# Third graph layer: 64-row halves of the array for a unit's sums and its image's sums, the 65th column apart

## What is computed

```python
log_ij = _logmap(x[:, None, :], x[None, :, :], c)
agg = jnp.einsum('ij,ijc->ic', adj / deg, log_ij)
transformed = agg @ weight + bias
return _expmap(jnp.zeros_like(transformed), transformed, c)
```

## Time and profile before

| what | value |
|---|---|
| three runs | 1090.72, 1091.84, 1092.6 us, median 1091.84 |
| profiled execution, its own time | 1090.43 us |
| its span, first to last instruction | 1088.7 us |
| PE busy | 1036.7 us (95%), 5430 passes |
| DVE busy | 862.8 us (79%) |
| ACT busy | 767.5 us (71%) |
| mean granted clock of PE | 0.987 |

### The profile page before, as it was taken

One profiled execution on the slowest core, in us unless ns is written; L12 is line 12 of the kernel. 1 busy time (PEld: TensorE's weight loads), 2 busy tenths in 40 slices (PEclk: granted clock), 3 DMA queues, 4 the chain that ended last, 5 costly groups with the idle time before them and its releaser, 6 DMA issues.

```text
span 1088.7 us, 14887 instructions
## 1 busy us (share of the span) xinstructions
PE 1036.7 (95%) x5430; PEld 448.2 (41%) x5430; DVE 862.8 (79%) x1013; ACT 767.5 (71%) x807; POOL 270.7 (25%) x140
## 2 busy tenths in 40 slices
PE   7999999999789999999979999999999998989998
PEld 2333333336633333334324443444554554436544
DVE  7999989996766666697669987887789887898781
ACT  5555455553556656676688899988888888997682
POOL 1089500000010000003015364434343433440010
PEclk9999999999989999999999999999999999999999
DMA  9989989980048888778754445555455545446451
GB/s 353 396 343 423 393 322 346 359 331 30 2 154 274 280 290 280 247 274 288 245 180 136 135 135 175 177 172 193 155 168 181 170 140 174 136 140 208 140 173 40
DMA packets 96341, 238.32 MB, mean 219 GB/s; under 512 B 16400, under 2 KB 45072, under 8 KB 79888
## 3 DMA queue, kind: packets, MB, share of 16 engines
q1 hardware_dynamic: 87056, 220.62, 58.3%
q10 hardware_dynamic: 9216, 16.78, 4.0%
HBM read 219.55 MB, written 17.83 MB: 218 GB/s over the span
## 4 chain that ended last, share of the span: by engine, by line
PE 74%; DVE 12%; ACT 9%; issue 4%; DMA 1%; SPq 0%; DVEq 0%; ACTq 0%
PE PS L563 51%; PE PS L737 5%; PE PS L738 5%; PE PS L870 4%; PE PS L839 4%; ACT work L1224 2%; ACT work L1232 2%; DVE work L1969 2%; DVE work L1957 1%; ACT work L1235 1%; DVE ring L1975 1%; DVE work L1963 1%; ACT work L1218 1%; PE PS L575 1%; ACT work L1155 1%
## 5 line engine op out<-in xcount | busy, mean ns | idle before, releaser
L1637 DVE TENSOR_TENSOR work<-work,ring 128x1024 f32<-128x1024 f32 x128 | 151.2, 1223 | 76.8 <-ACT work L1155 76.7
L1155 ACT ACTIVATE work<-PS,att_sc 128x1024 f32<-128x1024 f32 x128 | 147.7, 1202 | 85.7 <-PE PS L738 78.4
L1090 ACT ACTIVATE work<-PS 128x1024 uint8<-128x1024 f32 x128 | 124.0, 1020 | 107.6 <-PE PS L563 107.6
L563 PE MATMUL PS<-ring,work 128*65 128x256 f32 (+1 forms) x600 | 191.8, 467 | 4.1 <-DVE work L1996 4.0
L541 POOL TENSOR_TENSOR ring<-work,ring 128x1024 f32<-128x1024 f32 x57 | 135.9, 2384 | 236.6 <-DVE work L1969 236.5
L563 PE MATMUL PS<-work 128*64 128x512 f32 (+2 forms) x800 | 153.6, 526 | 1.1 <-ACT work L1218 1.0
L1963 DVE SCALAR_TENSOR_TENSOR work<-PS,work 128x1024 f32<-128x1024 f32 x72 | 88.0, 1223 | 53.8 <-PE PS L563 45.3
L563 PEld LDWEIGHTS PS<-ring,work 128*65 128x65 f32 x600 | 80.8, 139 | 91.5 <-issue 66.0
L737 PE MATMUL PS<-work 128*128 128x512 f16 x256 | 98.9, 386 | 2.0 <-DVE work L1444 1.3
L1224 ACT ACTIVATE work<-work 128x1024 f32<-128x1024 f32 x72 | 76.0, 1055 | 34.8 <-DVE work L1957 34.7
L738 PE MATMUL PS<-work 128*128 128x512 f16 x256 | 98.2, 384 | 0.0
(11 more groups left out here) (267 smaller groups left out, 1479.9 us busy)
## 6 DMA issues: line engine op xcount, KB each, us to landing
ring<-in_adj_t SPq DMA_DIRECT2D x96, 1024.0 KB, 5.3
ring<-in_adj_t SPq DMA_DIRECT2D x104, 512.0 KB, 3.8
work<-in_adj_t SPq DMA_DIRECT2D x32, 1024.0 KB, 8.3
codes<-work ACTq DMA_DIRECT2D x64, 256.0 KB, 7.4
ring<-codes SPq DMA_DIRECT2D x64, 256.0 KB, 3.7
H<-in_adj_t SPq DMA_DIRECT2D x24, 512.0 KB, 3.9
X<-in_x SPq DMA_DIRECT2D x2, 256.0 KB, 4.5
X<-in_x SPq DMA_DIRECT2D x1, 512.0 KB, 9.9
```

Source lines behind the costliest of these rows:

```text
L563: return mm(out_ap, lhsT, rhs, start=starts, stop=True, skip_group_check=True)
L1090: nc.scalar.activation(made[:, k, u * UNIT:(u + 1) * UNIT], PS[:, (4 + 2 * u) * BANK:(6 + 2 * u) * BANK], ACT.Relu).then_inc(sem("codes_ma ...
L1155: nc.scalar.activation(att[:, u, :], PS[:, (4 + 2 * u) * BANK:(6 + 2 * u) * BANK], ACT.Sigmoid, bias=att_sc[:, 2:3], scale=att_sc[:, 1:2]) ...
L1637: V.tensor_tensor(prob[:, m % 4, :], att[:, u, :], ring[:, s % RING, u * UNIT:(u + 1) * UNIT], ALU.mult)\
```

## The change

A unit's near sums go to PSUM rows 0 to 63 of bank 2, its image's sums to rows 64 to 127 of bank 3, each product with 64 stationary columns instead of 65, and the two kinds alternate in program order. The 65th column gets products of its own with one stationary column: for a unit four near ones of 256 moving columns (rows 0 and 32 of the upper half of bank 3), for an image eight of 128 columns (rows 64 and 96). GA then keeps near sums in rows 0 to 63 and far sums in rows 64 to 127, and DVE adds up the 65th column apart (33 rows). `nodes2` adds the two halves with a stacked identity (made once by POOL) and fetches the 65th column with products of one moving column, one for each tile below 4 and two for each other tile. `turn_left(1)` moves from bank 3 to bank 0.

```diff
+        stacked = sb("stacked", [P, D])
...
+        GU = (work[:, 11 * UNIT:12 * UNIT], TA[:, 2 * UNIT:3 * UNIT])
+        LAST = 3 * BANK + PAIR
+        def last_near(S):
+            return GU[S // (NS // 2)][0:33, S % (NS // 2) * PAIR:(S % (NS // 2) + 1) * PAIR]
+        def last_far(p):
+            return GU[p // NS][64:97, p % NS * P:(p % NS + 1) * P]
+        def last_rows(t):
+            S, p = t // ST, t // 2
+            r = 32 * (t % ST // 2)
+            rows = [(r, GU[S // (NS // 2)][:, S % (NS // 2) * PAIR + t % 2 * P:S % (NS // 2) * PAIR + (t % 2 + 1) * P])]
+            if t >= ST:
+                r = 64 + 32 * (t % 2)
+                rows.append((r, GU[p // NS][:, p % NS * P:(p % NS + 1) * P]))
+            return rows
...
+            nc.gpsimd.tensor_tensor(stacked[:, :], ident[:, 0:D], ident[:, D:P], ALU.add).then_inc(sem("consts_ready"), 1)
...
-            pe.wait_ge(sem("consts_ready"), 6)
+            pe.wait_ge(sem("consts_ready"), 7)
...
                 if n == AUX_L:
-                    pe.wait_ge(sem("far_out"), mirrors(n - 1))
-                    turn_left(1, 3)
+                    pe.wait_ge(sem("aux_r_out_a"), 2)
+                    turn_left(1, 0)
...
                 if n > AUX_R and mirrors(n) == mirrors(AUX_R) + 1:
-                    pe.wait_ge(sem("aux_r_out_a"), 2)
+                    pe.wait_ge(sem("aux_l_out"), 2)
                     pe.wait_ge(sem("aux_r_out_v"), 2)
...
-            def gather2_near(n):
+            def gather2(n):
...
+                if mirrored(n):
+                    pe.wait_ge(sem("far_ready"), mirrors(n))
+                if mirrors(n) - mirrored(n) > 0:
+                    pe.wait_ge(sem("far_out"), mirrors(n) - mirrored(n))
                 for q in range(2):
-                    ins = add(PS[0:D + 1, 2 * BANK:3 * BANK], Zn[:, 2 * p + q, 0:D + 1], near(n)[:, q * BANK:(q + 1) * BANK],
-                              opens(n) and q == 0)
+                    add(PS[half_rows(0), 2 * BANK:3 * BANK], Zn[:, 2 * p + q, 0:D], near(n)[:, q * BANK:(q + 1) * BANK],
+                        opens(n) and q == 0)
+                    if mirrored(n):
+                        for i in (2 * q, 2 * q + 1):
+                            add(PS[half_rows(1), 3 * BANK:LAST], Zn[:, S * ST + i, 0:D], far(n)[:, i * PAIR:(i + 1) * PAIR], i == 0)
+                for q in range(2):
+                    if mirrored(n):
+                        last_far2(n, 2 * q)
+                    for c in range(2):
+                        ins = add(PS[32 * c:32 * c + 1, LAST:LAST + PAIR], Zn[:, 2 * p + q, D:D + 1],
+                                  near(n)[:, q * BANK + c * PAIR:q * BANK + (c + 1) * PAIR], opens(n) and q == 0)
...
+                        ins = last_far2(n, 2 * q + 1)
...
+            def last_far2(n, i):
                 S, p = UNITS[n]
...
-                for i in range(ST):
-                    ins = add(PS[0:D + 1, 3 * BANK:3 * BANK + PAIR], Zn[:, S * ST + i, 0:D + 1], far(n)[:, i * PAIR:(i + 1) * PAIR], i == 0)
-                ins.then_inc(sem("agg2_far"), 1)
+                for c in range(2):
+                    ins = add(PS[64 + 32 * c:65 + 32 * c, LAST:LAST + P], Zn[:, S * ST + i, D:D + 1],
+                              far(n)[:, i * PAIR + c * P:i * PAIR + (c + 1) * P], i == 0)
+                return ins
 
             def nodes2(q):
                 pe.wait_ge(sem("near_out"), segments(COMPLETE[q]))
                 for t in range(*GROUPS[q]):
-                    ins = mm(PS[:, agg2_col(t):agg2_col(t) + D + 1], GA[0:D + 1, t * P:(t + 1) * P], ident[0:D + 1, 0:D + 1],
-                             start=True, stop=True)
+                    r, to = (P, stacked) if t >= ST else (D, ident)
+                    mm(PS[:, agg2_col(t):agg2_col(t) + D], GA[0:r, t * P:(t + 1) * P], to[0:r, 0:D], start=True, stop=True)
+                    for k, (r, rows) in enumerate(last_rows(t)):
+                        ins = add(PS[:, agg2_col(t) + D:agg2_col(t) + D + 1], rows, ident[:, r:r + 1], k == 0)
...
-                    one("aux_l_out", aux_l[:, UNIT:2 * UNIT], banks(3, 4).bitcast(BF16), ACT.Copy, ("aux_turned", 4))
+                    one("aux_l_out", aux_l[:, UNIT:2 * UNIT], banks(0, 1).bitcast(BF16), ACT.Copy, ("aux_turned", 4))
...
             def far2_out(n):
...
+                at, got = GA[half_rows(1), p * PAIR:(p + 1) * PAIR], PS[half_rows(1), 3 * BANK:LAST]
+                last, last_got = last_far(p), PS[64:97, LAST:LAST + P]
                 dve.wait_ge(sem("agg2_far"), mirrors(n))
+                dve.wait_ge(sem("agg2_near"), n + 1)
...
+                    V.tensor_tensor(at, at, got, ALU.add)
+                    V.tensor_tensor(last, last, last_got, ALU.add).then_inc(sem("far_out"), 1)
...
             def near2_out(n):
...
+                last, last_got = last_near(S), PS[0:33, LAST:LAST + PAIR]
                 dve.wait_ge(sem("agg2_near"), n + 1)
-                if n < N0 and S == 0:
+                dve.wait_ge(sem("agg2_far"), mirrors(n))
+                if n < N0 or S >= NS // 2:
+                    V.tensor_copy(last, last_got)
                     V.tensor_copy(at, got).then_inc(sem("near_out"), 1)
                 else:
-                    dve.wait_ge(sem("far_out"), mirrors(n))
+                    V.tensor_tensor(last, last, last_got, ALU.add)
                     V.tensor_tensor(at, at, got, ALU.add).then_inc(sem("near_out"), 1)
```

More of the change, by code:

```diff
@@ L937, in gather2_near @@
                     pe.wait_ge(sem("near_out"), segments(n))
+                if mirrored(n):
+                    pe.wait_ge(sem("far_ready"), mirrors(n))
+                if mirrors(n) - mirrored(n) > 0:
+                    pe.wait_ge(sem("far_out"), mirrors(n) - mirrored(n))
                 for q in range(2):
-                    ins = add(PS[0:D + 1, 2 * BANK:3 * BANK], Zn[:, 2 * p + q, 0:D + 1], near(n)[:, q * BANK:(q + 1) * BANK],
-                              opens(n) and q == 0)
-                ins.then_inc(sem("agg2_near"), 1)
@@ L943, in gather2_far @@
-            def gather2_far(n):
-                S, p = UNITS[n]
[L945 to L949, removed]
-                for i in range(ST):
-                    ins = add(PS[0:D + 1, 3 * BANK:3 * BANK + PAIR], Zn[:, S * ST + i, 0:D + 1], far(n)[:, i * PAIR:(i + 1) * PAIR], i == 0)
-                ins.then_inc(sem("agg2_far"), 1)
+                    add(PS[half_rows(0), 2 * BANK:3 * BANK], Zn[:, 2 * p + q, 0:D], near(n)[:, q * BANK:(q + 1) * BANK],
+                        opens(n) and q == 0)
@@ new lines, in gather2 @@
+                    if mirrored(n):
[7 more added lines that the diff above has]
+                                  near(n)[:, q * BANK + c * PAIR:q * BANK + (c + 1) * PAIR], opens(n) and q == 0)
+                    if q:
+                        ins.then_inc(sem("agg2_near"), 1)
+                    if mirrored(n):
+                        ins = last_far2(n, 2 * q + 1)
+                        if q:
+                            ins.then_inc(sem("agg2_far"), 1)
@@ L980, in _ @@
                 if n >= 2:
-                    gather2_near(n - 2)
-                    if mirrored(n - 2):
-                        gather2_far(n - 2)
+                    gather2(n - 2)
                 if n in FLIPS:
@@ L987, in _ @@
                 last_passage2(n)
-            gather2_near(NU - 2)
+            gather2(NU - 2)
             pe.wait_ge(sem("sum_ready"), NU)
@@ L1007, in last_passage3 @@
                 if q == 2:
-                    gather2_near(NU - 1)
+                    gather2(NU - 1)
                 if q == 3:
@@ L1978, in far2_out @@
                 S, p = UNITS[n]
-                at = GA[0:D + 1, p * PAIR:(p + 1) * PAIR]
-                got = PS[0:D + 1, 3 * BANK:3 * BANK + PAIR]
+                at, got = GA[half_rows(1), p * PAIR:(p + 1) * PAIR], PS[half_rows(1), 3 * BANK:LAST]
+                last, last_got = last_far(p), PS[64:97, LAST:LAST + P]
                 dve.wait_ge(sem("agg2_far"), mirrors(n))
+                dve.wait_ge(sem("agg2_near"), n + 1)
                 if S == 0:
-                    V.tensor_copy(at, got).then_inc(sem("far_out"), 1)
-                else:
-                    V.tensor_tensor(at, at, got, ALU.add).then_inc(sem("far_out"), 1)
+                    V.tensor_copy(at, got)
+                    V.tensor_copy(last, last_got).then_inc(sem("far_out"), 1)
+                else:
+                    V.tensor_tensor(at, at, got, ALU.add)
+                    V.tensor_tensor(last, last, last_got, ALU.add).then_inc(sem("far_out"), 1)
             def near2_out(n):
                 S, p = UNITS[n]
-                at = GA[0:D + 1, S * STRIP:(S + 1) * STRIP]
-                got = PS[0:D + 1, 2 * BANK:3 * BANK]
+                at, got = GA[half_rows(0), S * STRIP:(S + 1) * STRIP], PS[half_rows(0), 2 * BANK:3 * BANK]
+                last, last_got = last_near(S), PS[0:33, LAST:LAST + PAIR]
                 dve.wait_ge(sem("agg2_near"), n + 1)
```

(6 more changed lines are left out.)

## The result

The changed kernel takes 1122.3 us (median of 4 runs, 1120.84 to 1123.42), the kernel before 1092.2 beside it (4 runs, 1090.72 to 1092.84): ratio 1.0275, 95% interval 1.0256 to 1.0294. It is slower, as forecast, but by 30 us, not 12, and outside the range of 1093 to 1112. Its profiled execution has a span of 1120.8 us (before 1088.7) and a mean granted clock of 0.971 (before 0.987).

A forecast was written before the change was run, and what follows sets the result against it. PE (TensorE) bounds the middle of the third layer, DVE or ACT other parts. Third layer -12.2, nodes2 +14.3, fourth-layer head +2.5, clock +5.5 and +3.4 sum to +13.5 on 1090.43: 1104 us, range 1093 to 1112.

The forecast's parts named there:

- the gather with an image: PE's gather products for a unit with an image in the third layer: 2.96 us, 0.57 less than before.
- the period of 5.27 in the middle: Third-layer iterations at 700 to 780, where PE is the bound: period 5.27 us instead of 5.85.
- overlap at unequal lengths: Near and far gather passes overlap; rival says not: 1120 us, chance 0.10 shared with one-column gather products dearer than 1.6 us.
- the price of a pass in nodes2: Each nodes2 pass is set by its 128-column load: 0.11 us at full clock, twice that at 1.2 GHz.
- The third rival: nodes2's one-column passes cost 0.06 us or less, down to 1085.5 us; chance 0.11 together with a better third layer.
- the clock holds: Rival: nodes2's new stretches don't lower the granted clock; sum +4.6, 1095 us; chance 0.17.
- the head of the fourth layer: Gathers of units 70 and 71 get 1.06 longer each, near2_out a second instruction: +2.5 us.
- The last group's own work at full clock: 64 more passes in nodes2(2), the last group, at 0.11 us each: +7.0 us.
- The term for the clock: Half clock in nodes2(2), +5.5 us, and one low stretch of 3.4 us behind each of the first two groups, +3.4.
- DVE gets 0.2 longer per image: DVE's new 33 x 128 addition per image in the third layer: 0.2 us behind another; below 0.1, above 0.28.
- the stretches from 577.33 and 788.04: Third-layer stretches to 637.71 and 901.24, where DVE is near full or fills some iterations: -0.5 and -5.0 us.
- The stall at turn_left(1): Unit 14's transposes wait 2.25 us for ACT's copy; with own gathers +2.5 for 637.71 to 679.90, below 1, above 4.

The follow-up runs named there:

- e1: Changed kernel with nodes2 alone taken back to one product of 65 moving columns per tile (values not the layer's): 1090.6 us.
- e2: Kernel before, with one or two further one-column products of zeros per tile in nodes2: 1115.3 us.
- e4: Changed kernel with fewer nodes2 passes: one product with two moving columns fetches the 65th column of two tiles: 1099.5 us.
- e8: e4 with two wide bf16 filler products on PE ahead of the transposes of units 4 to 11: 1099.8 us.
- e6: e4 with turn_left(1) three units later (17 instead of 14) and the second flip of rows at 19 instead of 18: 1093.5 us.
- e7: e4 without DVE's addition of an image's 65th column (values not the layer's): 1095.2 us.
- e11: e4 plus e6's edit, nodes2's last group split around step 3, and halves swapped (image sums on rows 0 to 63): 1090.6 us, 0.9975 of the kernel before.
- e3: Changed kernel with a wide bf16 product (384 moving columns, 512 in the last group) behind each one-column product of nodes2: 1115.4 us.
- e9: e4 plus e6's edit, nodes2's last group split around step 3, and one semaphore wait instead of two in far2_out and near2_out: 1093.4 us.

## Why the forecast was wrong

**Right:** the direction; the gather with an image (2.96 forecast, 2.85 measured); the period of 5.27 in the middle, where 14 iterations gained 7.5; overlap at unequal lengths, so that rival is out, although the measured time lies in its band (1114 and more) and not in mine; the price of a pass in nodes2 at either level of the clock. The third rival, cheap passes, is out by the same rows. That the clock holds is out too. For units 24 to 41 without nodes2 I had -9.5, e1 shows -8.8; for the head of the fourth layer +2.5 against e1's +1.2, which is low by a fall of the clock that e1 lacks. The last group's own work at full clock was forecast at +7.0, and 16 x 0.67 - 3.7 = +7.0.

The miss of 18.6 (32.1 - 13.5, spans) has three parts, 8, 10 and 2, and a rest of about -1.5: +1.1 ahead of unit 0, +0.6 in units 1 to 5 and +0.7 in 24 to 41, against -0.8 in 59 to 71, -1.6 of unit 23 and -1.3 for the head of the fourth layer.

**The term for the clock, 8.9, was mis-sized: some 8 too small.** I took for the low stretch behind a group the length that one had in the earlier trace rows, 3.4 us. The rows after have 10.24, 10.24 and 17.07. For the first group: its tiles at full clock would take 2.63 + 4 x 0.67 = 5.3; it took 7.82, and the iteration behind it, mostly at 0.50, took 7.58 instead of 5.26, another 2.3. That is 4.8 for a forecast of 1.7. The group's stage costs 8.0 over e1 instead of 5.5, the second 7.9 instead of 5.2, the third 15.2 instead of 12.5. The step that failed is the length. I had named the level and the place of the falls; a single low stretch in the trace before was no evidence for the length of one behind longer thin work. Nor is the number of such products enough for it: e2 has as many in the first two groups and 6.8 us, and one and the same last group had 6.8 us in e4 and e8 and 3.4 in e6 and e7. The four executions of the changed kernel, with mean clocks of 0.971 to 0.974, don't differ much.

**The step "DVE gets 0.2 longer per image" failed, and with it the stretches from 577.33 and 788.04: 10 us.** Forecast -0.5 and -5.0, measured +3.5 and (e1) +1.0. The 0.2 was right for the short operation alone (e11: 600.72 to 600.92), but not with what the rows bring. It adds 0.32 when the next one can't overlap its end (600.06 to 600.38), and the first one starts 0.11 late, since the sums moved to rows 64 to 127. Sum operation to sum operation, an image in the way, is 600.38 - 598.47 = 1.91; before it was 1.47 (595.95 to 597.42): 0.44 per image, of which 0.24 are the two gaps (e11). DVE's busy time grew by 4.5 us over units 41 to 54 (70.71 before, 75.25 after). And I counted iterations that have room on DVE one by one; its work slides from one into the next, so where single pieces fill it every other iteration, PE's gain in the one is waited for in the next. From unit 41 to 42 PE gains 0.59, from 42 to 43 it loses 1.40 (5.85 and 6.92 before, 5.26 and 8.32 after). e7 and e11 take the addition and the gaps away singly and get 2.0 and 1.9 us back in 41 to 54: there the cause is shown.

For the stretch from 577.33 it is not. e7 and e11 get 0.7 and 0.9 back of the 3.5. What failed there is the step that PE and DVE alone bound it: 1.8 us of it arise where PE waits for POOL's preparation (e7 above), and POOL's work in the third layer had no term in the sum. How much of POOL's lateness comes from DVE's longer work stays open. Earlier in the same stretch `rest2` was also caught by POOL once:

```profile
589.13 2.37 POOL L528 TENSOR_TENSOR X<-X,work 128x1024 f32<-128x1024 f32 x1
```

```profile
589.69 2.36 DVE L1995 TENSOR_SCALAR work<-work 128x1024 f32<-128x1024 f32 x1
```

It took 2.36 us where it takes 0.68 alone. Before the change the same two met, and there POOL's instruction was the longer one (4.14 us) and `rest2` took 0.68; the next `rest2` took 1.03. The Trainium skill ("SBUF — State Buffer", Who interferes with whom) says that of a DVE instruction in a two-port mode and one on GpSimd the first to issue has the shared ports for its whole length and the other waits. The lengths agree, each time one of the two is longer, and in the row above `rest2` ends 0.55 behind POOL's; which one waits can't be told from the recorded starts, for POOL's is the earlier one here, before the change and in e11 (where it takes 4.34 and `rest2` 0.68, and the next `rest2` 1.78). No run here takes these meetings away, so the 1.3 us that I put on them in the stretch (1.68 - 0.35) stay argued.

**The stall at turn_left(1) was mis-sized: +4.5 instead of +2.5 in units 15 to 23,** above my upper bound of 4 for the stretch. The wait was as I read it, 2.28 us against 2.25. What I hadn't priced is the fall of the clock behind the pause, at 652.9, with 4.54 instead of 2.89 for the own unit's gather. e6 takes both away. Unit 23, which I had left out of every stretch, gave 1.6 back.

The 0.6 us in units 1 to 5 I had costed at nothing; no run here isolates them. The kernel before has a low stretch of 6.8 us there and the changed one only 3.4; e6 and e7, with 6.8, come to +1.9. What sets the length of a low stretch, and why the clock falls near 618 in most versions with the change and not in the kernel before, stays open.

## What to carry to other kernels

A gather that runs on two halves of the array gets its time, but what was one operand with 65 columns is now two, and each consumer pays: count the products of a thin operand by the load, and the vector engine's pieces by start to start in place, not by their width. Give every engine a term, also the one that looks idle: single pieces of its work can be what TensorE waits for. Don't line up many one-column products: let one product pick several columns, and put streaming work between groups. When two halves of the partitions are to be had, give rows 0 to 63 to the one whose results the vector engine reads most often, if its instructions before and behind begin at row 0.

## What the runs showed of the hardware

- The granted clock went to 0.50 in stretches in which the profile has PE busy all the time (17.23 of 17.23 us, PEld 17.21) with loads of 128 columns and 1 to 64 moving ones. In e3 it stayed at 1.00 when each one-column product had a 512-column one behind it (15.06 of 15.06 us busy), at a price of 12.6 us for the last stage instead of 16.4.
- Low stretches in and behind these groups were 3.4 us long (before, e6, e7), 6.8 (e2, e4, e8), 10.2 (changed kernel), 13.7 (e2) and 17.1 (changed kernel). The same group had 3.4 in one execution and 6.8 in another.
- A pass of nodes2 took 0.11 us at a granted clock of 1.00 and 0.21 at 0.50 (changed kernel). A wide bf16 product behind each one-column product added 0.13 us (e3: 0.93 for a tile with two instead of 0.67), so the loads ran in part beneath it.
- On DVE a neighbour's overlap of 0.08 us turns into a gap of 0.03 where the rows begin at 64 on one side and at 0 on the other (changed kernel, e9; gone in e11); a second semaphore wait ahead of an instruction cost nothing (e9).
- A DVE instruction of 0.68 us took 2.36 beside one of POOL (changed kernel), and POOL's of 2.37 took 4.34 in the same meeting in e11.
- One-column products on four groups of rows and passes of 512 beside pairs of 256 columns overlapped: 36 passes in 2.85 us, where the streaming alone, overlapped in full, comes to 2.58 (changed kernel).
